# Cross attention in a two-layer decoder: weighing at the end of each slot, one maximum folded away, output products in other slots, a mean moved to ScalarE

## The reference

```python
q = rms_norm((x @ Wq.T).reshape(b, 256, 16, 128), q_norm_w)          # 16 query heads
kv_in = concat([context, x], axis=1)                                 # 1601 + 256 = 1857 keys
k = rms_norm((kv_in @ Wk.T).reshape(b, 1857, 4, 128), k_norm_w)      # 4 key/value heads
v = (kv_in @ Wv.T).reshape(b, 1857, 4, 128)
q, k = rope(q, positions_q), rope(k, positions_k)
scores = einsum('bhqd,bhkd->bhqk', q, repeat(k, 4)) * 128 ** -0.5
out = softmax(scores) @ repeat(v, 4)
return out.reshape(b, 256, 2048) @ Wo.T
```

## Time and profile before

| what | us |
|---|---|
| median of 3 runs | 1730.97 |
| lowest, highest | 1723.27, 1736.09 |
| the profiled execution | 1732.53 |
| its span, first to last instruction | 1730.7 |

### The profile page before, as it was taken

One profiled execution on the slowest core, in us unless ns is written; L12 is line 12 of the kernel. 1 busy time (PEld: TensorE's weight loads), 2 busy tenths in 40 slices (PEclk: granted clock), 3 DMA queues, 4 the chain that ended last, 5 costly groups with the idle time before them and its releaser, 6 DMA issues. The chain is left out here.

```text
span 1730.7 us, 26027 instructions
## 1 busy us (share of the span) xinstructions
PE 1517.4 (88%) x8324; PEld 878.2 (51%) x8324; DVE 1338.3 (77%) x2706; ACT 1014.7 (59%) x2343; POOL 1147.3 (66%) x1068
## 2 busy tenths in 40 slices
PE   6597796766798999999899999989989999999697
PEld 5476464533454554545455454545545555454354
DVE  7875577878687888888788878878887888888554
ACT  3363564652566666666666666666656666666342
POOL 2363470132577789888688977867998777886542
PEclk9799798879899999999999999999999999999889
DMA  3000820010000001000000000000000000000010
GB/s 97 1 2 13 303 88 25 1 70 0 32 13 1 13 13 39 1 1 1 1 1 13 27 1 1 1 1 1 21 19 1 1 1 1 1 1 1 7 49 26
DMA packets 30945, 38.49 MB, mean 22 GB/s; under 512 B 4948, under 2 KB 26456, under 8 KB 30808
## 3 DMA queue, kind: packets, MB, share of 16 engines
q1 hardware_dynamic: 30808, 36.82, 6.6%
HBM read 35.76 MB, written 1.05 MB: 21 GB/s over the span
## 5 line engine op out<-in xcount | busy, mean ns | idle before, releaser
L2136 POOL TENSOR_TENSOR stream_acc<-stream_acc,stream_weights 128x512 f32<-128x512 f32 (+1 forms) x404 | 523.6, 1296 | 135.6 <-ACT stream_weights L2042 119.8
L1979 PE MATMUL stream_banks<-stream_weights,stream_v 128*128 128x512 f32 (+1 forms) x872 | 458.8, 610 | 37.3 <-ACT stream_weights L2042 36.3
L2036 ACT COPY stream_weights<-stream_banks 128x512 f32<-128x512 f32 (+1 forms) x436 | 256.5, 588 | 263.3 <-PE stream_banks L1947 260.1
L2206 DVE TENSOR_TENSOR stream_most<-stream_most,stream_banks 128x512 f32<-128x512 f32 x448 | 304.9, 681 | 79.4 <-ACT stream_weights L2036 71.9
L2042 ACT ACTIVATE stream_weights<-stream_weights 128x512 f32<-128x512 f32 (+1 forms) x436 | 277.0, 636 | 110.4 <-DVE stream_weights L2194 107.6
L2194 DVE TENSOR_TENSOR stream_weights<-stream_weights,stream_banks 128x512 f32<-128x512 f32 (+1 forms) x436 | 295.1, 679 | 3.2 <-PE stream_banks L1968 1.8
L1979 PEld LDWEIGHTS stream_banks<-stream_weights,stream_v 128*128 128x128 f32 (+1 forms) x872 | 159.1, 191 | 132.6 <-ACT stream_weights L2042 81.9
L1947 PE MATMUL stream_banks<-stream_q_t_hi,stream_k_t_hi 128*128 128x512 bf16 (+1 forms) x480 | 183.6, 383 | 9.9 <-DVE stream_most L2206 8.6
L1947 PE MATMUL stream_banks<-stream_q_t_lo,stream_k_t_hi 128*128 128x512 bf16 (+1 forms) x480 | 183.1, 381 | 0.0
L1947 PE MATMUL stream_banks<-stream_q_t_hi,stream_k_t_lo 128*128 128x512 bf16 (+1 forms) x480 | 183.0, 381 | 0.0
L2143 POOL TENSOR_TENSOR stream_by_cos<-stream_by_cos,stream_by_sin 128x256 f32<-128x256 f32 x192 | 135.0, 725 | 50.0 <-DVE stream_by_sin L2234 49.8
(11 more groups left out here) (436 smaller groups left out, 3114.3 us busy)
## 6 DMA issues: line engine op xcount, KB each, us to landing
memory_raw_t<-in_ctx_t SPq DMA_DIRECT2D x4, 1601.0 KB, 9.0
memory_raw<-in_ctx SPq DMA_DIRECT2D x4, 1536.0 KB
row_ctx_t<-in_ctx_t SPq DMA_DIRECT2D x6, 512.0 KB, 3.6
early_raw<-in_L_xattn_Wq SPq DMA_DIRECT2D x4, 512.0 KB, 3.9
early_raw<-in_L_xattn_Wo SPq DMA_DIRECT2D x4, 512.0 KB, 3.9
row_ctx_t<-in_ctx_t SPq DMA_DIRECT2D x1, 1601.0 KB, 8.0
moe_raw_up<-in_L_ffn_wi SPq DMA_DIRECT2D x6, 256.0 KB, 4.3
model_x<-in_x SPq DMA_DIRECT2D x1, 1024.0 KB, 5.5
```

The lines of the kernel that those rows point to most:

```text
L1979: nc.tensor.matmul(ps[:, 2 + n, :], v[0:r, g % 2, t, :], room(step)[0:r], start=(t == 0), stop=(t == KT - 1)).then_inc(weighed, 1)
L2036: nc.scalar.copy(room(step)[0:r], ps[0:r, step % 2, :]).then_inc(copied, 1)
L2136: nc.gpsimd.tensor_tensor(acc[0:r, h % 2, :], acc[0:r, h % 2, :], room(step)[0:r], ALU.add).then_inc(acc_ready, 1)
L2206: nc.vector.tensor_tensor(most[0:r], most[0:r], ps[0:r, step % 2, :], ALU.max).then_inc(maxed, 1)
```

## The change

Five edits, all in the cross attention:

- On TensorE `weigh` comes last in each slot, and `project` directly behind `score`.
- `keep_most` does nothing for the first step of a pass; for the second it takes the maximum of the room with the first step's scores and the bank with the second's. The counts of `maxed` shift by one per pass (`maxima`), and the scores that reuse the first step's bank wait for ScalarE's copy.
- `take_top` moves on VectorE from slot 0 of the next pass to slot 1, behind the rotations; the maximum of a slot comes behind it.
- The output products and their additions move from slots 36 and 39 after a pass began to 38 and 40 (slots 8 and 10 of 15). The last pass keeps its slot.
- `vary` goes from VectorE (behind the last rotation) to ScalarE (behind the squares of a query unit, or behind the values of a key unit's second part), as an Identity activation with 1e-6 as bias from a new tile `eps`.

```diff
+OUT_LATE = 2 * STEPS + 8
@@ outs_in
-        found += [(h, m) for h in pass_at(slot, SUM_LATE + (1, 4)[m]) if h < PASSES - 1]
+        found += [(h, m) for h in pass_at(slot, OUT_LATE + 2 * m) if h < PASSES - 1]
@@ cross_attention
+        eps = sb("eps", [P, 1])
+                    nc.gpsimd.memset(eps[:], 1e-6)
@@ cross_stream
+        def maxima(step):
+
+            return step - step // STEPS
@@ score
-                    if step >= 2:
-                        pe.wait_ge(maxed, step - 1)
+                    if step >= 2 and (step - 2) % STEPS == 0:
+                        pe.wait_ge(copied, step - 1)
+                    elif step >= 2:
+                        pe.wait_ge(maxed, maxima(step - 2))
@@ TensorE's list
                     if 0 <= slot < ALL:
                         score(slot)
-                    if 0 <= slot - WEIGH < ALL:
-                        weigh(slot - WEIGH)
+                    for e in range(4):
+                        for u in units_at(slot, e):
+                            project(u, e)
                     for h in pass_at(slot, TOPS_LATE):
                         turn_most(h)
...
-                    for e in range(4):
-                        for u in units_at(slot, e):
-                            project(u, e)
                     for u in turns_in(slot):
                         turn(u)
...
                     for h, m in outs_in(slot):
                         project_out(h, m)
+                    if 0 <= slot - WEIGH < ALL:
+                        weigh(slot - WEIGH)
@@ ScalarE
+                def vary(u, n):
+                    heads = slice(0, width(u))
+                    if u >= 2:
+                        ac.wait_ge(rms_ready, u - 1)
+                    ac.wait_ge(squared, part_at[(u, n)] + 1)
+                    nc.scalar.activation(var[:, u % 2, heads], ss[:, u % 2, heads], ACT.Identity, bias=eps[:, 0:1],
+                                         scale=1.0 / HD).then_inc(var_ready, 1)
@@ ScalarE's list
                             take_values(u, 0)
+                        else:
+                            vary(u, 0)
...
                             take_values(u, 1)
+                            vary(u, 1)
@@ VectorE: keep_most
+                    if t == 0:
+                        return
                     ve.wait_ge(copied, step + 1)
-                    if t == 0:
+                    if t == 1:
                         if h >= 1:
                             ve.wait_ge(most_turned, h)
-                        nc.vector.tensor_copy(most[:], ps[:, step % 2, :]).then_inc(maxed, 1)
+                        nc.vector.tensor_tensor(most[:], room(step - 1), ps[:, step % 2, :], ALU.max).then_inc(maxed, 1)
@@ VectorE's list
                     for u in units_at(slot, 3):
                         rotate(u, 0)
-                        if unit(u)[1] < QT:
-                            vary(u)
                     for u in units_at(slot, 6):
                         if unit(u)[1] >= QT:
                             rotate(u, 1)
-                            vary(u)
+                    for h in pass_at(slot, TOPS_LATE + 1):
+                        take_top(h)
                     if 0 <= slot < ALL:
                         keep_most(slot)
-                    for h in pass_at(slot, TOPS_LATE):
-                        take_top(h)
```

More of the change, by code:

```diff
@@ L1702, in _, with cross_stream @@
                                                 own_t[0][:, :, tok], ALU.subtract)
-        cross_stream(nc, x, const, a, w, experts, w_q, w_kv, w_o, k_gain, q_gain, freq, ones, own, half, own_t, in_t, ctx_t,
+        cross_stream(nc, x, const, a, w, experts, w_q, w_kv, w_o, k_gain, q_gain, freq, ones, own, half, eps, own_t, in_t, ctx_t,
                      where, where_f, angle, turns, sin, k_tab, q_tab, kept["raw"])
-def cross_stream(nc, x, const, a, w, experts, w_q, w_kv, w_o, k_gain, q_gain, freq, ones, own, half, own_t, in_t, ctx_t,
+def cross_stream(nc, x, const, a, w, experts, w_q, w_kv, w_o, k_gain, q_gain, freq, ones, own, half, eps, own_t, in_t, ctx_t,
                  where, where_f, angle, turns, sin, k_tab, q_tab, raw):
@@ L1951, in turn_most @@
                 def turn_most(h):
-                    pe.wait_ge(maxed, STEPS * (h + 1))
+                    pe.wait_ge(maxed, maxima(STEPS * (h + 1) - 1))
                     wait_bank6("tops", h)
@@ L2198, in keep_most @@
                     r = rows_of(t)
+                    if t == 0:
+                        return
                     ve.wait_ge(copied, step + 1)
-                    if t == 0:
+                    if t == 1:
                         if h >= 1:
                             ve.wait_ge(most_turned, h)
-                        nc.vector.tensor_copy(most[:], ps[:, step % 2, :]).then_inc(maxed, 1)
+                        nc.vector.tensor_tensor(most[:], room(step - 1), ps[:, step % 2, :], ALU.max).then_inc(maxed, 1)
                     else:
-                        ve.wait_ge(maxed, step)
+                        ve.wait_ge(maxed, maxima(step - 1))
                         nc.vector.tensor_tensor(most[0:r], most[0:r], ps[0:r, step % 2, :], ALU.max).then_inc(maxed, 1)
@@ L2234, in rotate @@
                     nc.vector.tensor_tensor(by_sin[:, u % 2, some], heads, tab[1], ALU.mult).then_inc(taken, 1)
-                def vary(u):
-                    n = width(u)
-                    if u >= 2:
-                        ve.wait_ge(rms_ready, u - 1)
-                    nc.vector.tensor_scalar(var[:, u % 2, 0:n], ss[:, u % 2, 0:n], 1.0 / HD, 1e-6, ALU.mult, ALU.add).then_inc(var_ready, 1)
                 def low(u):
```

## The result

The changed kernel takes 1706.56 us (median; 1705.79 to 1708.44) against 1731.08 us (1723.27 to 1736.09) for the kernel before, measured beside it: a ratio of 0.9865, 95% interval 0.9832 to 0.9898. That is 24.5 us between the medians, 1.4% faster, and 0.6 us from the forecast. So close a hit is luck: several terms of the sum were wrong and cancelled.

A forecast was written before the change was run, and what follows sets the result against it. TensorE's queue bounds the kernel, with about 3.6 of some 4.4 us lost per group in slots 5 to 14. Terms of -44.1, +6.8, +3.2, +12.0 and smaller ones sum to -25.7: 1732.5 becomes 1706.8, stated as 1706 us, range 1684 to 1730.

The forecast's parts named there:

- Slots 5 to 14 of a regular group: Stretch with a TensorE hole of 3.6 us; 3.15 us saved per group, times 14 is -44.1 us.
- The product of slot 23 waiting for `low`: Slots 21 to 25: TensorE reaches product 0 before low ends and stands 1.0 us; +0.86 us net, times 14 is +12.0.
- ScalarE as host of the mean: The mean of squares on ScalarE takes 0.25 us plus a wait for the last square, 0.3 us together.
- Rival (a): Gain in slots 5 to 14 full (-3.5 x 14), new waits small, losses a third: 1685 us; chance 0.12.
- Rival (b): Two rotations still hold slots 6 and 11, slots 5 to 14 save only 2.0 us: 1721 to 1727 us; chance 0.27.
- Rival (c): ScalarE becomes the chain; a late mean delays next copy, maximum and score: +34 us, 1765 us; chance 0.08.
- rival (d): ScalarE loads a table before and after each of 92 means, 235 us of ScalarE: 1850 us; chance 0.02.
- Slots 0 to 2: TensorE's turned top waits for take_top behind slot 1's rotations: +0.86 us there, +0.75 net, times 9 is +6.8.
- Slot 16: TensorE ready at 928.75, take_top done at 929.0: +0.2 us with the earlier 0.1 gap, times 16 is +3.2.
- Table groups: Groups 1, 3, 5, 7, 9, 11: no change in slots 0 to 2; adjustments +2.4, -1 x 3 and -1.5 x 2.
- The fold: Dropping 32 first-maximum copies of 0.69 us from VectorE mostly buys nothing, since it stood idle 41.6 us before them.
- The mean: In slot 6 on VectorE the mean of squares takes 1.17 us ahead of the maximum; median 0.16, worst 1.18.

The follow-up runs named there:

- top_slot0: The changed kernel with take_top back in slot 0 of the next pass on VectorE: 1697.72 us, ratio 0.9802.
- b_weigh_last: The kernel before with only TensorE's order changed (projections behind the scores, weighing last): 1710.41 us, ratio 0.9882.
- weigh_second: The changed kernel with the weighing back directly behind the scores, ahead of projection, turns and products: 1698.10 us, ratio 0.9812.

## Why the prediction was right, and where it was not

**Right, with their sizes.** Slots 5 to 14 of a regular group (-3.15 said, -3.37 measured in group 6): the turn of slot 7 no longer waits for additions, score 13 no longer waits, the weighing finds its exponentials. But the sum credits chiefly the mean and the additions, and gives the weighing's place one sentence; alone, that place makes the largest part (-2.70, against -1.97 for the mean and -1.39 for the products, group 13). The turned top waiting behind rotations (0.86 said, 0.92 in the row). The product of slot 23 waiting for `low` (+0.86 said, +0.95 in the regular groups, +0.72 in group 6, which had 12.15 instead of 11.91 before). ScalarE as host of the mean: 0.30 us said, 0.296 to 0.328 measured with a median of 0.304, 0.20 until the next instruction starts (933.85 to 934.05). Rival (a) had the gain there nearly full, and so it was, but the new waits came as well. Rival (b), the rotations alone holding slots 6 and 11, did not come. Rival (c), ScalarE as the chain, did not come: it is busy 14.80 of 20.85 us in slots 5 to 14, and TensorE's waits for its exponentials fell from 47 to 7; only its split of the turned tile stands in the new wait of slot 23. No new table loads, rival (d): four at the exponentials' line, as in the earlier trace rows.

```profile
L2069 ACT ACTIVATE stream_var<-stream_ss,cross_eps x96: 296/304/328, 443.5 to 1532.6; 128x4 f32<-128x4 f32 x80, 128x3 f32<-128x3 f32 x16
...
L2051 ACT ACT_TABLE_LOAD x4 | 5.1, 1283 | 0.1
```

The Trainium skill, "ScalarE: Activation LUTs" (Table sets), has identity in every set; this trace now agrees. The prediction's estimate of 0.28 us, which comes out of that page's formula for an activation with a bias operand ("What ACT_TABLE_LOAD costs"), lies beside a measured 0.304.

**Mis-sized terms.** Slots 0 to 2: +0.75 said, +0.96 measured. Slot 16: +0.2 said, +0.43 measured. There take_top ends 0.29 us after TensorE is ready (0.25 was drawn), but the turned top starts 0.14 us later still (918.16 against 918.02), and the weighing behind it takes 0.96 us to the next score (918.31 to 919.27) instead of 0.86; the sum had neither. Slots 18 to 20: +0.08, not in the sum. The product of slot 8 was to start 0.4 late; it starts some 0.2 late (at 900.22, where the projection before it began at 899.81 and takes 0.21). So a regular group saves 0.93 us (group 13) to 1.3, where the sum had 1.34: eight of them 9.1 us instead of 10.7.

**Table groups.** The sum took -16.1 us from the six; they gave 9.1. The step that failed is that slots 5 to 14 save what a regular group saves: there they save 14.4 us in all (171.5 to 157.1), not the 18.9 that I took (6 x 3.15) with another 6 for VectorE's chain and the slow clock. Groups 7 and 11 save 3.7 and 3.6 us, group 3 only 0.5, groups 1, 5 and 9 together 6.6. What I set at nothing, slots 0 to 2, gave 1.7, and slots 3 and 4 gave 2.1. In groups 3, 7 and 11 a sign that I had listed under "wrong" did come, GpSimd late with normalising. The turns of slots 7 and 12 wait for it, 0.96 and 0.82 us; in group 3, GpSimd, then TensorE:

```profile
677.48 0.83 POOL L2174 TENSOR_TENSOR stream_normed<-stream_by_cos,stream_rms 128x384 f32<-128x384 f32 x1
```
```profile
678.36 0.55 PE L1941 MATMUL stream_banks<-model_ident,stream_normed 128*128 128x128 f32 x3 [0.96 <-POOL stream_normed L2174]
```

Slots 5 to 14 of these three take 23.7 us, against 20.85 in a regular group. In top_slot0, group 7 has neither of the two waits and takes 21.55.

**The end.** Left out of the sum, and worth -3.4 us; with group 0 and group 15 (-0.8 and -0.9, where I had +1.2 for both) and 0.8 before the stream it filled the gap: -18.2 inside, -5.9 outside, -24.1 in the span, where the sum had -26.9 inside and +1.2 outside. That these errors cancel is luck. After the last score there are no scores behind which an exponential can be late, so the weighing's place in the list decides. TensorE before, then after:

```profile
1607.24 1.12 PE L1979 MATMUL stream_banks<-stream_weights,stream_v 128*128 128x512 f32 x2 [0.88 <-ACT stream_weights L2042]
1608.30 0.39 PE L1968 MATMUL stream_banks<-stream_flat,cross_own 4*128 4x128 bf16 x4
```
```profile
1586.25 0.39 PE L1977 MATMUL stream_banks<-stream_flat,cross_own 4*128 4x128 bf16 x4
```

Before, a weighing that waits for its exponential holds up the spread, on which the next pass's lowering and exponentials hang: it comes 6.7 us after the last score (1601.63) instead of 5.3 (1580.96). The last matmul of the output products starts 35.3 us after the last score in the kernel before and 32.0 in the changed one; b_weigh_last, with nothing but the order changed, has 32.4, and weigh_second, with everything but the order, 34.4. So the order makes most of it. What follows takes 93.8 and 93.7 us in the two; that the ends of the kernels with the new order still differ from 122.3 to 126.4 us lies mostly there, in the unchanged code and its granted clock.

**The fold.** I wrote that most of it buys nothing, since VectorE stood idle before those copies. That is true of the old order. In the new one take_top comes behind that copy on the same engine, and TensorE waits for it: 18.5 us. The step read the idle time before the removed work and did not ask what the same change puts behind it.

**The mean.** I gave its 1.17 us the weight of a property of the kernel. The runs show that it depends on whether GpSimd's addition has begun. The rule I cited from the Trainium skill ("SBUF — State Buffer", the section on the two sides) says the same, that whoever starts first holds the pair; the rows agree, 0.16 us in the gap and 1.17 beside an addition. I used it for the cause and not for the consequence.

**Why parts that give 20 each give 24 together.** Mean, products and order alone give 22, 19 and 20 us. They shorten one and the same chain, by which rotations, maximum and additions come late in slots 6 to 13: once it has slack, a second remedy finds little (slots 5 to 14: 22.24, 22.82 and 21.51 alone, 20.85 with all). The losses in slots 0 to 2, 15 to 17 and 21 to 25 lie in different places and do not overlap in this way. Group 13 of the changed kernel (69.55) is longer than with any of the three alone (68.70, 69.08, 68.65). The fold alone and take_top in slot 1 alone were not tried on the kernel before; only their removal from the changed one was.

## What to carry to other kernels

In an engine's in-order list, put work that is ready ahead of work that waits: an instruction moved last is cover lost for whatever waits ahead of it (here up to 0.9 us a time). When several edits attack one chain, try each alone and leave each out: gains overlap, losses add, and the best set need not be the whole. Price a stall between two engines as a coincidence that any shift in time can make or remove, and add up the end of the pipeline too, where there is no further work to hide behind.

## What the hardware showed

- A four-column mean on VectorE took 0.16 us between two GpSimd additions and 1.15 to 1.20 us just behind the start of one; the 35 long ones of the kernel before all ended 0.02 to 0.03 us after the GpSimd instruction beside them. The same 96 instructions took 47.7, 37.0, 29.4 or 25.4 us in four kernels that differ in the order and place of other work.
- With take_top back in slot 0 (top_slot0), TensorE's granted clock fell to 0.50 around one wait of 2.56 us (matmuls of 0.63 instead of 0.38 us), and stayed at 1.00 in the changed kernel, where 2.44 us of waiting came in two pieces with work between. It also stayed at 1.00 around another wait of 2.56 us, four groups later in the same run. So removing a short wait ahead of a long one can cost more than it saves, but these runs give no rule for when.
- The same code behind the last output product took 90.4 to 91.3 us at a mean granted clock of 0.91 to 0.93, and 93.7 to 94.0 us at 0.88 to 0.90.
